# A last product of squares issued behind the next group's first low-rank products, and VectorE's scaling moved behind its statistics and first low part

## The reference, cut to what matters

```python
# x: (4, 2048, 256) float32, 8192 tokens of 256 features
x = x + attention(_layernorm(x))              # window 128 and one global key, 16 heads, then @ Wo.T
x = x + ffn(_layernorm(x))

def ffn(x, fast_b, w_fc, w_proj, u, v, gate): # hidden 1024, rank 16
    h = _bitlinear(x, w_fc) + gate * (x @ v.T @ fast_b.T @ u.T)
    r = jnp.maximum(h, 0.0)
    return _bitlinear(r * r, w_proj)

def _bitlinear(x, w_latent):                  # ternary weights times one scale per row
    scale = clip(mean(abs(w_latent), axis=1), 1e-05)
    return x @ (clip(round(w_latent / scale), -1, 1) * scale).T
```

## Time and profile before

| | |
|---|---|
| three timed runs | 1077.13, 1082.81 and 1084.80 us, median 1082.81 |
| the profiled execution | 1076.39 us, of which 1074.1 us span from the first to the last instruction |
| busy over the span | PE 96%, PEld 73%, DVE 86%, ACT 72%, POOL 65% |
| granted TensorE clock | 0.992 over the span, 1.00 from 718 us to the end |
| stage_feed, first to last step | 706 to about 1074 us: a first step of 24.12 us, 13 of 23.07 us, one of 20.19 us and the last group's |

### The profile page before, as it was taken

The page is one execution under the profiler, slowest core; times in us unless marked ns, Lnnn a source line. Parts: engine busy times, 40 slices in busy tenths (PEclk is TensorE's granted clock), DMA queues, the critical chain, the costliest instruction groups (busy, mean ns, idle before and its releaser), DMA issues.

```text
span 1074.1 us, 40075 instructions
## 1 busy us (share of the span) xinstructions
PE 1031.9 (96%) x16071; PEld 787.8 (73%) x16071; DVE 924.8 (86%) x3205; ACT 775.0 (72%) x1326; POOL 698.4 (65%) x947
## 2 busy tenths in 40 slices
PE   8999999799999999999999999799999999999997
PEld 8888887356655666567655665478888888888886
DVE  7789986899989999999989998578888888888885
ACT  6999987587888888887888878654556555556554
POOL 2585556688988888888889888743344443334443
PEclk9999999899999999999999999999999999999999
DMA  6999989767667866786687753502123111123001
GB/s 196 254 316 279 289 232 266 163 131 154 134 127 162 154 125 140 156 152 127 134 163 142 141 102 68 178 1 80 59 78 99 60 59 60 59 75 93 31 21 39
DMA packets 185289, 142.32 MB, mean 132 GB/s; under 512 B 59896, under 2 KB 184848, under 8 KB 185104
## 3 DMA queue, kind: packets, MB, share of 16 engines
q1 hardware_dynamic: 185104, 139.77, 54.6%
HBM read 87.98 MB, written 50.95 MB: 129 GB/s over the span
## 4 chain that ended last, share of the span: by engine, by line
PE 61%; DVE 12%; issue 4%; ACT 2%; SPq 1%; DMA 1%; POOL 1%; POOLq 0%; DVEq 0%
PE e_psum L1627 13%; PE e_psum L1649 12%; PE e_psum L1359 9%; PE e_psum L1909 6%; PE e_psum L1911 6%; DVE a_masked L1374 4%; PE e_psum L1891 3%; PE e_psum L1890 3%; DVE n_stats L146 2%; DVE f_x L2031 2%; PE e_psum L1895 1%; PE e_psum L259 1%; PE e_psum L257 1%; PE e_psum L258 1%; PE e_psum L1859 1%
## 5 line engine op out<-in xcount | busy, mean ns | idle before, releaser
L1699 ACT ACTIVATE a_weights<-e_psum 128x1024 f32<-128x1024 f32 (+1 forms) x512 | 391.5, 809 | 80.2 <-PE e_psum L1627 79.8
L1374 DVE CUSTOM_DVE_ANT_0 a_masked<-e_psum,band 128x290 f32<-128x290 f32 (+1 forms) x992 | 387.5, 445 | 33.7 <-PE e_psum L1359 27.9
L1538 POOL TENSOR_SCALAR_AFFINE_SELECT a_weights<-a_weights 128x1024 f32<-128x1024 f32 x256 | 273.2, 1091 | 43.3 <-ACT a_weights L1699 42.0
L1953 POOL TENSOR_TENSOR f_square<-f_relu 128x512 f32<-128x512 f32 x128 | 146.2, 1143 | 209.5 <-ACT f_relu L1942 187.9
L1359 PE MATMUL e_psum<-e_k,e_q 96*32 96x290 bf16 (+2 forms) x4096 | 235.0, 286 | 14.2 <-DVE max L1374 6.4
L1627 PE MATMUL e_psum<-e_q,e_k 128*32 128x384 bf16 (+2 forms) x5632 | 240.4, 279 | 5.8 <-ACT a_weights L1699 3.8
L1649 PE MATMUL e_psum<-a_weights,a_v 128*17 128x384 f32 (+2 forms) x2816 | 222.0, 392 | 5.4 <-DVE e_turned L1412 5.1
L1627 PEld LDWEIGHTS e_psum<-e_q,e_k 128*32 128x32 bf16 x5632 | 130.4, 96 | 97.7 <-ACT a_weights L1699 44.1
L1359 PEld LDWEIGHTS e_psum<-e_k,e_q 96*32 96x32 bf16 x4096 | 115.9, 97 | 82.8 <-DVE max L1374 46.9
L1909 PE MATMUL e_psum<-w_w_t,f_square_hi 128*128 128x256 f32 x512 | 129.4, 287 | 5.7 <-DVE f_square_lo L2007 5.7
L1911 PE MATMUL e_psum<-w_w_t,f_square_lo 128*128 128x256 f32 x512 | 126.7, 282 | 0.0
(11 more groups left out here) (220 smaller groups left out, 1934.0 us busy)
## 6 DMA issues: line engine op xcount, KB each, us to landing
k_parts<-p_k_parts SPq DMA_DIRECT2D x48, 258.0 KB, 5.0
e_k<-k_parts SPq DMA_DIRECT2D x64, 193.5 KB, 4.1
q_parts<-p_q_parts SPq DMA_DIRECT2D x48, 256.0 KB, 5.9
e_q<-q_parts SPq DMA_DIRECT2D x64, 192.0 KB, 4.0
v_ones<-p_va SPq DMA_DIRECT2D x16, 544.0 KB, 6.3
e_k<-k_parts SPq DMA_DIRECT2D x64, 129.0 KB, 3.5
p_x<-in_x SPq DMA_DIRECT2D x16, 512.0 KB, 7.1
e_q<-q_parts SPq DMA_DIRECT2D x64, 128.0 KB, 3.9
```

The lines of the kernel that those rows point to most:

```text
L1374: dve.tensor_tensor_reduce(out=masked[:, place + lo:place + hi], in0=bank[:, lo:hi], in1=self.band[:, lo:hi], scale=1.0, scalar=NEG, op0=A ...
L1538: pool.affine_select(out=blocks, in_=blocks, compare_op=ALU.is_ge, fill=0.0, base=0, pattern=[[0, NQ // 2 * HEAD_COLS // P // CUT_STEP], [ ...
L1699: act.activation(pe_w[:, us.upar, lo:hi], score[c % 2][:], ACT.Exp).then_inc(s_exp, 1)
L1953: pool.tensor_tensor(sh.r2[:, j % 4, :], sh.r[:, j % 4, :], sh.r[:, j % 4, :], ALU.mult).then_inc(self.s_sq, 1)
```

## The change

Three edits, all in the order in which `stage_feed` issues; no instruction is added, removed or changed in size.

1. TensorE: block 7 of `pe_output` of the group before (now `qb`) is issued after the next group's `pe_low_rank`, `pe_ternary` 0 and 1 and `pe_low` 0 and 1, instead of ahead of them. For the very last group it stays where it was.
2. VectorE: `dve_scaled` (two instructions) goes from the head of the step to behind `dve_square_low` of block 0.
3. VectorE: `dve_final` (two instructions) goes from behind `dve_z_low` to behind `dve_square_low` of block 1. So `dve_z_low` opens the step and `dve_front` follows it.

```diff
@@ block.tensor @@
+            if qf and qb:
+                feed.pe_output(pe, qb, MH - 1)
             if qa:
                 feed.pe_turn_o(pe, qa, qf)
...
-            elif qf:
-                feed.pe_output(pe, qf, MH - 1)
@@ block.vector @@
             if qb and qb.g == G - 1:
                 feed.dve_last(dve, qb)
-            elif qb:
-                feed.dve_scaled(dve, qb)
             if qf:
                 feed.dve_z_low(dve, qf)
-            if qb and qb.g < G - 1:
-                feed.dve_final(dve, qb)
             if qx:
                 feed.dve_front(dve, qx)
...
             for j in range(MH):
                 if qf:
                     feed.dve_square_low(dve, qf, j)
+                if j == 0 and qb and qb.g < G - 1:
+                    feed.dve_scaled(dve, qb)
+                if j == 1 and qb and qb.g < G - 1:
+                    feed.dve_final(dve, qb)
                 if j == 1 and qx:
                     norm.rstd(dve, qx)
```

More of the change, by code:

```diff
@@ L2078, in body @@
         def body(at):
-            qa, qx, qf = at(0), at(LX), at(LF)
+            qa, qx, qf, qb = at(0), at(LX), at(LF), at(LB)
             if qf:
```

## The result

| | before | after |
|---|---|---|
| median of nine timed runs each | 1079.99 us | 1087.9 us |
| lowest to highest | 1076.54 to 1084.80 | 1086.21 to 1091.89 |
| profiled execution (its span) | 1076.39 (1074.1) | 1086.58 (1084.8) |

The changed kernel takes 1.0072 of the time of the one before, with a 95% interval of 1.0049 to 1.0095: 7.9 us slower. Predicted were 1087.3 us and +7.0.

A forecast was written before the change was run, and what follows sets the result against it. TensorE, busy 96% of the span, was taken to bound the kernel. Thirteen steps' 6.2 us plus 0.4 for each of the last two groups gave 7.0, added to the 1080.3 mean: 1087.3 us, range 1076 to 1097.

The forecast's parts named there:

- The ceiling: Third stage: with nothing else late, TensorE's removed waits gain at most 9.7 us, 0.9%.
- The two terms of the sum: TensorE's waits removed: 14 places of 0.58 us for block 0's low part, plus 1.6 us in the last two groups.
- Block 0 is in time, and z was never late: Step's head: L2000 still starts at 1.75; block 0's L2007 ends at 5.82, ready by 7.42 with 1.6 us to spare.
- L157, the squares, the first L2031: VectorE beside GpSimd's squares: L157 held to 5.05, first L2031 to 9.09, its pair ending at 9.70, costing 0.84 more.
- The hold on the tiny instructions: VectorE ahead of block 2's low part: L169 held to 10.61, L171 gets by, L173 held by square 4 to 11.75.
- Block 2's product: TensorE wants block 2's low part at 11.65, starts at 12.60: 0.95 late plus 0.11, a loss of 1.06 a step.
- The sum: Third stage: +0.48 a step over 13 steps is 6.2 us, plus 0.4 for each of the last two groups: 7.0 us.
- The wait for the relu: Last two groups: second-stage products wait 0.70 us for block 0's relu, plus some 0.1; the moved matmuls fill this hole.
- the low bound of +3: If L173 and L175 passed unheld, block 2's L2007 ends at 12.28: +0.2 a step, +3 us.
- rival 3: VectorE beside squares 4 and 5: L175 or block 2's L2007 meets another whole square, +11 to +15 us; chance 0.20.
- rival 2: VectorE's L2031 is not held by squares: steps of 22.49 us, -9.7 to -7 us; chance 0.14.

## Why the prediction was right, point by point

- **The ceiling.** 9.7 us were to be had if nothing became late. The kernels without the new wait come near it: -8.6 us with L2031 behind block 5, steps of 22.42 where 22.49 were expected. The two terms of the sum were off in opposite ways. The 13 steps give 0.65 each instead of 0.58, 8.5 us in all. The last two groups were to give 1.6 and give some 0.1: TensorE no longer waits for the relu of block 0, but waits 0.42 for block 6's low part and 0.58 for L1994 (the normalised rows' low part) instead.
- **Block 0 is in time, and z was never late.** Right: L2000 starts 874.43 - 872.68 = 1.75 into the step, as before and as worked out; block 0's low part ends at 5.83 (5.82 worked out).
- **L157, the squares, the first L2031.** Right to about a tenth: L157 ends at 5.06 (5.05), L2031's pair at 9.80 (9.70). What comes behind is 0.11 late, because L2013 followed its forerunner 0.72 after its start (877.82 to 878.54) where I had 0.61: it began 0.03 behind the end of L2007, while others begin 0.08 ahead of the end of the one before.
- **The hold on the tiny instructions.** The size was right, the instruction was not: L171 was held (0.97), where I had let it by and held L173. L171 was asked for at 10.75 instead of 10.64, and square 4 stands at 10.66 (883.34) where I had 10.69, so the square was now the first. Whichever meets that square pays for it, which is why the sum did not suffer.
- **Block 2's product.** Predicted at 12.60, measured at 12.79. The loss of a step is 1.17 + 0.10 against 1.06; the step 23.69 against the 23.5 foretold.
- **The sum.** +0.48 a step were +0.62; 13 steps give 8.1 instead of 6.2. For the last two groups I had +0.4 each without working them out. The last but one took +0.85 (20.19 to 21.04 us). From the last group's first L1881 to the end lie 23.86 us before and 25.23 after, of which 0.96 is the moved product of the group before, so the last group lost 0.4. The wait for the relu is gone in both, as foretold; what came in its place are waits of 1.28 and 0.61 for block 2's low part and one of 0.31 for L1994 between them.
- **The time.** In all the two profiled executions differ by 9.4 us within the stage, where 7.0 were worked out; the medians differ by 7.9 (5.3 to 10.3). That 1087.3 met 1087.9 within a microsecond is partly luck: the mechanism and the place were right, the size was a quarter too small by the trace. The range was loosely drawn as well: the low bound of +3 on the lowest execution gives 1079.4, not 1076, and a change of 0.7% could be told from none, where I had thought that it takes 1%.
- **The rivals.** No further hold came (rival 3), and L2031 was held (rival 2 is wrong; a kernel in which it is not held does give that rival's time). The Trainium skill (SBUF — State Buffer, section Who interferes with whom) has the one that issues first keep the port for the whole instruction. The trace agrees on who goes first, and not on "whole": the first L2031 of 880.35 takes 1.53 (the pair's 2.13 less the 0.60 by which the second is set off) and ends at 881.88, 0.55 behind the square's 881.33, while alone it takes 0.68. The recorded ends of GpSimd are rough, so this is a distance between records; when the port changes hands is not shown.

## What to carry to other kernels

An engine that is 85% busy and off the path sets the time as soon as its in-order run up to one early result is longer than the work that covers it. Follow that run instruction by instruction to each place where the bound engine picks something up, not only to the wait that is there now. Removing a wait of VectorE (17.4 us here) was worth nothing by itself, since L2000 then waited as long for z. When moving VectorE work with two SBUF inputs, or a tiny instruction of this kind, look what GpSimd does at the new place: the same pair costs 1.3 us beside an idle GpSimd and 2.1 beside a busy one.

## What had not been expected of the hardware

**A wait of TensorE can cost more than itself.** In the kernel with TensorE's edit and the least of VectorE's, every middle step has one wait of 2.45 us, for block 0's low part. Busy time by stretch, ahead of and behind the end of the one at 874.39 (the stretch, its us, then PE, PEld, DVE, ACT and POOL with their instructions, the granted clock, the DMA share and GB/s):

```profile
871.00:874.30 3.30, 0.93 (x5) 0.41 (x3) 3.23 (x13) 0.54 (x2) 0.00 (x0) 1.00 0.49 159
874.30:877.50 3.20, 3.11 (x13) 2.71 (x14) 3.06 (x9) 3.05 (x6) 1.89 (x2) 0.68 0.96 279
```

The clock is 1.00 while TensorE waits and 0.68 in the stretch after it, a mean over 2.4 and 1.2 GHz. TensorE's timeline shows where it falls:

```profile
874.39 0.39 PE L1909 MATMUL e_psum<-w_w_t,f_square_hi 128*128 128x256 f32 x1 [2.45 <-DVE f_square_lo L2007]
...
875.33 0.31 PE L1911 MATMUL e_psum<-w_w_t,f_square_lo 128*128 128x256 f32 x1
875.45 0.62 PE L1890 MATMUL e_psum<-f_xt_hi,w_w_t 128*128 128x512 f32 x1
875.86 0.63 PE L1891 MATMUL e_psum<-f_xt_lo,w_w_t 128*128 128x512 f32 x1
876.29 0.63 PE L1890 MATMUL e_psum<-f_xt_hi,w_w_t 128*128 128x512 f32 x1
```

One us after the wait ended, matmuls follow each other at 0.43 instead of 0.23 us, for some 3 us. That costs 26.7 - 25.15 = 1.55 us a step. In the ten steps that have it, the clock falls between 0.3 us before and 1.6 us after the end of the wait. The wait that ended at 901.11 was as long, 2.45, with the DMA engines as busy behind it (0.92), and no such fall followed, as in three of the 13 steps. The waits of 1.00 us in the changed kernel and of 1.25 us with VectorE's edits alone never had it. That the long wait brings the fall is argued from this comparison; what decides between the ten steps and the three is not shown.

**A 128x4 instruction can cost as much as a 128x512 one.** L157, L169, L171 and L173 take 0.16 to 0.17 us alone, and those of them that meet a square of 1.04 us take 0.73 to 1.03, in every middle step of the stage. L157 and L173 read one tensor only and are held all the same; L2013, which reads one from PSUM and one from SBUF, runs beside a square in 0.69 and is not.
